# A fused decoder layer: the running maximum of the memory cell by four broadcast DMAs, the causal mask on GpSimd, and straight code in place of a loop

## The chip, the cores and the metric

The kernel runs on one core of one Trainium2 chip. The metric is the device time of one execution in microseconds, as the median of three runs; lower is better. The engines are TensorE (PE, its weight loads PEld), VectorE (DVE), ScalarE (ACT), GpSimd (POOL) and SyncE (SP), whose queue (SPq) issues all DMAs here.

## What is computed

Sixteen sequences of 256 rows and 256 columns pass through one layer of three parts, each followed by a residual sum and a layer norm: softmax attention with 16 heads and a position bias; a memory cell (mLSTM) with 4 heads of 64, whose queries are the rows and whose keys and values are a second input; and a gated feed-forward part with quantised rows and ternary weights. The change is in the memory cell. The reference has there, cut:

```python
log_fg = jax.nn.log_sigmoid(fg)
cs = jnp.cumsum(log_fg, axis=2)
log_D = where(ltr, cs - swapaxes(cs, 2, 3), -inf) + swapaxes(ig, 2, 3)
max_log_D = jnp.max(log_D, axis=-1, keepdims=True)
D = jnp.exp(log_D - max_log_D)
C = (qh @ kh.T / sqrt(DH)) * D
normalizer = maximum(abs(sum(C, -1)), exp(-max_log_D))
h = C / (normalizer + EPS) @ vh
```

With a = ig - cs and m the running maximum of a, the exponent is a[t] - m[s] for t up to s, and nothing otherwise. So each head needs its row m, 256 numbers on one SBUF partition, spread over all 128 partitions.

## The kernel before, in words

The work of a sequence (called a batch, B is 16) is spread over four or five passes of one body, so that in one pass the engines serve batches n2 = b + 2 (projections), n = b + 1, b (attention scores and softmax), c = b - 1 (end of attention, gates of the memory cell), f = b - 2 (memory cell, begin of the feed-forward part), e = b - 3 (its end) and d = b - 4 (store). Each engine has a `body` (SP L331, POOL L505, PE L834, ACT L1149, DVE L1591) that is a list of steps in an order written out by hand; between the engines stand only semaphores. Every engine is in order, so a step that waits holds up all that stands behind it in its list.

`iterations` (L247) runs the bodies: passes -1 to 3 and 14 to 19 are straight code, passes 4 to 13 are five rounds of a hardware loop with two bodies in it (`Fori`, L251). At the end of a round each engine branches back; the loop's waits are against register values.

A softmax tile (one head, 128 of its 256 rows) goes through `scores` (PE, L582), `biased` (DVE, L1311: bias and row maximum), `negated` (row tile 0 on ACT L947, row tile 1 on POOL L434), `turned` (PE transposes, L598), `exponentials` (ACT, L959) and `values` (PE, L615). There are two PSUM banks for scores, two for the turned tiles, one for values, and three that all other products share in the order of the list `uses` (L208): `lease` makes a product wait until the last user of its bank is done.

The memory cell of a batch: `mem_gates` (PE) and `gate_rows`, `gate_logs` (ACT, L984, L997) give input and forget gates as 4 rows of 256. `forget_logs` (DVE, L1500) forms the log of the forget gate, `forget_sums` (L1507) its running sum, `input_rows` (L1516) a, `running_max` (L1523) m, `max_rows` (L1530) the exponents for the normalizer. Then m is cut into three bfloat16 parts: `max_high` (L1537), `max_rest` (L1544), `max_mid` (L1552), `max_low` (L1559) on DVE, and `max_mid_copy` (L1010) on ACT. For each head `mem_decay` (PE, L702 to L705) spreads -m over 128 partitions by a product of these parts with a selecting matrix, and adds -1e30 above the diagonal by two products of the identity with `causal`. `mem_weights` on ACT (L980, L981) takes the exponential out of PSUM with a as its bias, `mem_weights` on DVE (L1490) multiplies it into the product of `mem_scores` (PE, L717), and `mem_values` (PE, L734) follows. Later come `head_stats`, `head_moments`, `head_scale`, `head_norm` (DVE), `head_rstd`, `mem_scaled`, `mem_residual` (POOL), and the feed-forward part: `row_max` (DVE, L1393), `quantised_rows`, `rows_turned`, `gate_proj`, `up_proj`, `gated`, `gated_up`, `inner_max`, `inner_scale`, `scaled`, `inner_quantised`, `down`, `ffn_residual`.

SP issues per pass the store, the second input (`load_ctx`, L318), the rows two batches ahead (`load_x`, L311), twelve SBUF to SBUF transfers of 128 KB each that stack the parts of queries and keys into 16 partitions each (`load_stack`, L305), and the residual rows `xb` (`load_residual`, L324), to which POOL adds a bias (`residual_in`, L501) for `attention_residual` (DVE, L1588).

Of the kernel before, what the change touches and what calls it, by code (L numbers as in the profile page):

```python
# [21 lines left out]
XH, XD = 4, 64  # L22
# [35 lines left out]
def build(nc, x, ctx, Wq, bq, Wk, bk, Wv, bv, Wo, bo, pos_bias, ig_w, ig_b, fg_w, fg_b, norm_w,  # L58
          w_gate, w_up, w_down, out):
    es = ExitStack()  # L60
    with es:
# [3 lines left out]
        def sig(name, per_batch=1):  # L65
# [5 lines left out]
        causal = sb("causal", [P, P], BF16)  # L71
        magic = sb("magic", [P, 1])
        zeros = sb("zeros", [P, 1])
        minus_half = sb("minus_half", [P, 8])
        xhead_sel = sb("xhead_sel", [96, XH, P], BF16)
# [42 lines left out]
        mm = sb("mm", [XH, 2, S])  # L118
        md = sb("md", [XH, S], BF16)
        ms = sb("ms", [96, S], BF16)  # L120
        aT = sb("aT", [P, TT, XH])
        emT = sb("emT", [P, 2, TT, XH])
        dT = sb("dT", [P, 2, 3 * P])
# [65 lines left out]
        gt_ps, gt_a, gt_v, ms_a = sig("gt_ps"), sig("gt_a", 4), sig("gt_v", 9), sig("ms_a")  # L189
        am_ps, am_a = sig("am_ps"), sig("am_a", 2)  # L190
        ar_ps, qk_ps, d_sb, c_sb, cv_ps, cv_sb = (sig("ar_ps", XH), sig("qk_ps", XH), sig("d_sb", 2 * XH),
# [17 lines left out]
            ("u2", 3, h_v, 6), ("g3", 3, h_v, 7), ("u3", 3, h_v, 8), ("ar0", 2, d_sb, 2), ("qk0", 2, c_sb, 1),  # L209
            ("ar1", 2, d_sb, 4), ("qk1", 2, c_sb, 2), ("ar2", 2, d_sb, 6), ("qk2", 2, c_sb, 3), ("cv0", 2, cv_sb, 1),  # L210
            ("cv1", 2, cv_sb, 2), ("cv2", 2, cv_sb, 3), ("ar3", 2, d_sb, 8), ("qk3", 2, c_sb, 4),
            ("ott0", 1, att_v, 3), ("ott1", 1, att_v, 4), ("cv3", 2, cv_sb, 4), ("attT", 1, attT_sb, 1),
            ("wo", 1, ln1, 1), ("hq0", 3, hq_sb, 1), ("cxT", 1, cxT_sb, 1), ("hq1", 3, hq_sb, 2), ("v", -1, v_sb, 1),
            ("y0", 3, y_v, 1), ("x1T", 1, x1T_sb, 1), ("y1", 3, y_v, 2), ("xT", -2, xT_sb, 1), ("gates", 1, gt_a, 1),
            ("q", -2, q_f, 1), ("k", -2, k_f, 1), ("xqT", 2, xq_sb, 1), ("g0", 2, h_v, 1), ("u0", 2, h_v, 2),
            ("g1", 2, h_v, 3), ("u1", 2, h_v, 4), ("g2", 2, h_v, 5), ("am", 1, am_a, 2),
# [41 lines left out]
        G_ALL = 21  # L258
# [10 lines left out]
        def _(sp):  # L269
# [7 lines left out]
            sp.wait_ge(g_set.sem, 5)  # L277
# [17 lines left out]
            def load_stack(n, par, which):  # L295
# [3 lines left out]
                wait(sp, split, n, 4 * which + 4)  # L299
# [20 lines left out]

            def load_residual(b):
                if live(b):
                    wait(sp, ln1, b - 1, 1)
                    sp.dma_start(xb[:], x[b].rearrange("(t p) d -> p t d", p=P)).then_inc(xb_in.sem, 16)  # L324

            def store(e):
                if live(e):
                    wait(sp, out_g, e, 3)
                    sp.dma_start(out[e].rearrange("(t p) d -> p t d", p=P), ot).then_inc(o_out.sem, 16)

            def body(b, par=None):  # L331
                par = b % 2 if par is None else par
                n2, n, c, d = b + 2, b + 1, b - 1, b - 4
# [13 lines left out]
        def _(pool):  # L347
# [5 lines left out]
            step(pool.memset(causal[:], 0.0))  # L353
            step(pool.memset(gate_w[:], 0.0))
            step(pool.memset(gate_b[:], 0.0))
            pool.wait_ge(g_set.sem, 3)
# [3 lines left out]
            step(pool.affine_select(out=causal[:], in_=causal[:], compare_op=ALU.is_ge, fill=-1.0e30, base=0,  # L360
                                    pattern=[[1, P]], channel_multiplier=-1))
            step(pool.memset(ones, 1.0))
            step(pool.memset(zeros[:], 0.0))
            step(pool.memset(minus_half[:], -0.5))
            step(pool.memset(xhead_sel[:], 0.0))
            step(pool.memset(ms[:], 0.0))
# [4 lines left out]
            pool.wait_ge(g_set.sem, 12)  # L371

            n = 17
            for off in (0, 32, 64):
                n += 1
                step(pool.affine_select(out=xhead_sel[:], in_=xhead_sel[:], compare_op=ALU.not_equal, fill=-1.0,
                                        base=-off, pattern=[[-1, XH], [0, P]], channel_multiplier=1))
                pool.wait_ge(g_set.sem, n)
# [23 lines left out]
            def split_high(n, which):  # L402
# [9 lines left out]
                wait(pool, split, n, 4 * which + 1)  # L412
                pool.tensor_tensor(src, src, parts[:, 0, which, :, :], ALU.subtract).then_inc(split.sem, 1)  # L413

            def split_low(n, which):
# [4 lines left out]
                wait(pool, split, n, 4 * which + 2)  # L420
                apart(pool)
                pool.tensor_scalar(parts[:, 1, which, :, :], src, 1.0, 0.0, ALU.mult, ALU.add).then_inc(split.sem, 1)
                wait(pool, split, n, 4 * which + 3)
# [13 lines left out]
            def inner_quantised(f, t):  # L437
# [3 lines left out]
                wait(pool, hr_a, f, t + 1)  # L441
# [8 lines left out]
            def output(e):  # L450
# [6 lines left out]
                wait(pool, out_g, e, 1)  # L457
                pool.tensor_tensor(nb[:, 1, :], nb[:, 0, :], rs[:, 2, :], ALU.mult).then_inc(out_g.sem, 1)
                wait(pool, out_g, e, 2)
# [7 lines left out]
            def head_rstd(f):  # L467

                if not live(f):
                    return  # L470
                wait(pool, gn_v, f, 22)
                apart(pool)
                pool.tensor_scalar(nrm[:, 6, :, :], nrm[:, 5, :, :], 1e-5, None, ALU.add).then_inc(gn_g.sem, 1)
                wait(pool, gn_g, f, 1)
                pool.tensor_tensor(nrm[:, 7, :, :], nrm[:, 6, :, :],
                                   minus_half[:, 0:TT * XH].rearrange("p (t h) -> p t h", t=TT), ALU.pow)\
                    .then_inc(gn_g.sem, 1)

            def mem_scaled(f):
# [3 lines left out]
                wait(pool, gn_v, f, 31)  # L483
# [3 lines left out]
            def mem_residual(f, par):  # L487
# [3 lines left out]
                wait(pool, gn_g, f, 3)  # L491
                pool.tensor_tensor(y2[:], y2[:], x1[:, par, :, :], ALU.add).then_inc(gn_g.sem, 1)  # L492

            def residual_in(b):
# [5 lines left out]
                wait(pool, xb_in, b, 16)  # L500
# [4 lines left out]
            def body(b, par=None):  # L505
                par = b % 2 if par is None else par
                n2, n, c, f, e = b + 2, b + 1, b - 1, b - 2, b - 3
                inner_quantised(e, 1)
                negated(b, 8)
                head_rstd(f)  # L510
                rstd(c, 0)
                mem_scaled(f)
                mem_residual(f, par)
                negated(b, 9)
                negated(b, 10)
                rstd(f, 1)
                negated(b, 11)
# [1185 lines left out]
```

## Time and profile before

| what | value |
|---|---|
| median of three runs | 857.5 us (857.29 to 859.87) |
| the profiled execution | 857.06 us |
| its span, first to last instruction | 855.3 us |
| mean granted TensorE clock | 0.924 |
| busy share of the span | PE 85%, DVE 80%, ACT 73%, POOL 55% |

The busy shares are over the whole span, with some 105 us at the start and 65 us at its end in which the passes are not full. The view by stretches (windows) gives the busy time of each engine between two moments, and the clock that was granted. As marks serve the starts of `forget_sums` (L1507), which runs once in a pass.

### The profile page before, as it was taken

What the parts mean: (1) busy time and instruction counts of PE and PEld (TensorE: products, weight loads), DVE (VectorE), ACT (ScalarE), POOL (GpSimd) and SP (SyncE); (2) the same over time, 40 slices, a digit from 0 to 9 for tenths busy, and PEclk for the clock granted to TensorE, in tenths of its full rate; (3) what the DMA queues carried; (4) which work ended last, traced back from release to release, by engine and by line L of the source; (5) the groups of instructions that cost most, each with busy time, mean ns of one, the idle gap of its engine ahead of it and who ended that gap; (6) DMA issues with size and microseconds to landing.
All of it is one profiled execution on the core that took longest, in us unless ns stands there. A gap on an engine that the chain in (4) does not pass through costs nothing.

```text
span 855.3 us, 20244 instructions
## 1 busy us (share of the span) xinstructions
PE 730.9 (85%) x5424; PEld 540.7 (63%) x5424; DVE 685.3 (80%) x2517; ACT 624.1 (73%) x1284; POOL 470.5 (55%) x777
## 2 busy tenths in 40 slices
PE   3379998998989798998999798988999889895842
PEld 3367776776858485866768485857668675653411
DVE  4755577989898889987888889997888998886843
ACT  0437868888888779895978779895978887875522
POOL 3446446566666667563656666673656673535132
PEclk8589999999999899998989999998989998998756
DMA  8867305070606052520607061501607070000000
GB/s 256 180 103 114 51 18 95 11 103 14 113 13 113 13 89 34 82 42 28 84 13 111 13 100 23 104 19 40 72 13 111 13 99 15 26 13 13 14 13 12
DMA packets 54582, 51.19 MB, mean 60 GB/s; under 512 B 6117, under 2 KB 54250, under 8 KB 54506
## 3 DMA queue, kind: packets, MB, share of 16 engines
q1 hardware_dynamic: 54506, 50.38, 33.9%
q8 instruction: 23, 0.38, 0.2%
q14 instruction: 53, 0.43, 0.2%
HBM read 21.00 MB, written 4.19 MB: 29 GB/s over the span
## 4 chain that ended last, share of the span: by engine, by line
PE 44%; DVE 17%; ACT 15%; issue 12%; POOL 9%; SPq 1%; POOLq 1%; DVEq 1%; DMA 0%; ACTq 0%
PE pT L598 7%; PE pO L615 5%; PE pS L582 3%; PE pB L655 2%; PE pA L655 2%; ACT L1002 2%; DVE sc L1311 2%; ACT sc L947 2%; DVE st L1323 2%; PE pB L717 2%; PE pC L568 2%; PE pC L717 1%; POOL rs L395 1%; POOL y L492 1%; ACT att L1060 1%
## 5 line engine op out<-in xcount | busy, mean ns | idle before, releaser
L434 POOL TENSOR_SCALAR sc<-sc,mx 128x256 f32<-128x256 f32 x256 | 129.0, 508 | 190.8 <-DVE mx L1311 187.5
L1311 DVE CUSTOM_DVE_ANT_0 sc<-pS,bias 128x256 f32<-128x256 f32 x512 | 199.0, 417 | 40.0 <-PE pS L582 33.5
L598 PE MATMUL pT<-ident,sc 128*128 128x128 f32 x1024 | 159.3, 280 | 28.0 <-ACT sc L947 19.0
L959 ACT ACTIVATE pr<-pT 128x512 f32<-128x512 f32 x256 | 149.5, 597 | 31.3 <-PE pT L598 30.2
L598 PEld LDWEIGHTS pT<-ident,sc 128*128 128x128 f32 x1024 | 119.2, 143 | 63.8 <-ACT sc L947 39.3
L947 ACT ACTIVATE sc<-sc,mx 128x256 f32<-128x256 f32 x256 | 124.0, 507 | 0.6 <-DVE mx L1311 0.2
L582 PE MATMUL pS<-ks,qs 96*128 96x256 bf16 x512 | 97.1, 277 | 5.8 <-DVE mx L1311 5.7
L615 PE MATMUL pO<-pr,va 128*32 128x256 f32 x1024 | 76.4, 421 | 0.0
L582 PEld LDWEIGHTS pS<-ks,qs 96*128 96x128 bf16 x512 | 43.4, 99 | 34.5 <-DVE mx L1311 20.8
L446 POOL TENSOR_SCALAR hq<-h 128x512 bf16<-128x512 f32 x64 | 38.4, 617 | 44.1 <-ACT h L1137 43.8
L411 POOL TENSOR_SCALAR parts<-qk_f 128x512 bf16<-128x512 f32 x32 | 20.6, 644 | 67.7 <-ACT qk_f L1105 66.2
L969 ACT ACTIVATE oT<-pO 128x256 f32<-128x256 f32 x64 | 24.2, 378 | 36.2 <-PE pO L615 36.2
L1049 ACT ACTIVATE x<-y,shift,rs 128x256 f32<-128x256 f32 x64 | 34.8, 591 | 16.9 <-POOL shift L399 16.3
L615 PEld LDWEIGHTS pO<-pr,va 128*32 128x32 f32 x1024 | 28.5, 116 | 23.8 <-issue 12.2
L1137 ACT ACTIVATE h<-h,magic,hs 128x1024 f32<-128x1024 f32 x32 | 40.0, 1248 | 4.8 <-DVE hs L1470 4.8
L1323 DVE BATCH_NORM_STATS2 st<-y 128x6 f32<-128x256 f32 x96 | 36.1, 419 | 8.7 <-POOL y L492 7.5
L1311 DVE DVE_READ_ACCUMULATOR2_ANT mx<- 128x1 f32 x512 | 41.3, 81 | 0.0
L424 POOL TENSOR_TENSOR parts<-qk_f,parts 128x512 bf16<-128x512 f32 x32 | 38.7, 1210 | 2.7
L413 POOL TENSOR_TENSOR qk_f<-qk_f,parts 128x512 f32<-128x512 f32 x32 | 38.3, 1196 | 2.7
L1452 DVE TENSOR_REDUCE hs<-h 128x1 f32<-128x1024 f32 x32 | 38.8, 1213 | 0.0
L395 POOL TENSOR_TENSOR rs<-ve,minus_half 128x2 f32<-128x2 f32 x48 | 35.5, 740 | 1.4
L631 PE MATMUL pB<-xT,wqT 128*128 128x256 f32 x128 | 32.3, 397 | 2.8 <-ACT xT L1096 2.8
(282 smaller groups left out, 1925.4 us busy)
## 6 DMA issues: line engine op xcount, KB each, us to landing
qs<-parts SPq DMA_DIRECT2D x96, 128.0 KB, 4.5
ks<-parts SPq DMA_DIRECT2D x96, 128.0 KB, 6.0
xin<-in_x SPq DMA_DIRECT2D x16, 256.0 KB, 3.5
bias<-in_L_attn_pos_bias SPq DMA_DIRECT2D x4, 1024.0 KB, 20.4
xb<-in_x SPq DMA_DIRECT2D x16, 256.0 KB, 6.3
cx<-in_ctx SPq DMA_DIRECT2D x32, 128.0 KB, 2.1
out<-hq SPq DMA_DIRECT2D x16, 256.0 KB, 2.2
sc<-in_L_ffn_w_gate SPq DMA_DIRECT2D x1, 1024.0 KB, 5.6
```

The source lines that it names most:

```text
L395: pool.tensor_tensor(rs[:, which, :], ve[:, which, :], minus_half[:, 0:TT], ALU.pow)\
L424: pool.tensor_tensor(parts[:, 2, which, :, :], src, parts[:, 1, which, :, :], ALU.subtract)\
L434: pool.tensor_scalar(sc[:, s % RING, 1, :], sc[:, s % RING, 1, :], -1.0, mx[:, s % RING, 1:2], ALU.mult, ALU.add).then_inc(neg_g.sem, 1)
L582: ins = pe.matmul(pS[s % 2][:, t * S:t * S + S], qs[par][:, s, t * P:t * P + P], ks[par][:, s, :], start=True, stop=True)
L598: ins = pe.transpose(bank[:, kt * S + t * P:kt * S + t * P + P], sc[:, s % RING, t, kt * P:kt * P + P], ident[:])
L615: ins = pe.matmul(pO[32 * j:32 * j + 32, 0:S], va[par][:, kt, hd, :], pr[:, hd % RING, kt, :], start=(kt == 0), stop=(kt == TT - 1))
L947: act.activation(sc[:, s % RING, 0, :], sc[:, s % RING, 0, :], ACT.Identity, bias=mx[:, s % RING, 0:1], scale=-1.0).then_inc(neg_a.sem, 1)
L959: act.activation(flat(pr[:, s % RING, :, :]), pT[s % 2][:, :], ACT.Exp, scale=-1.0)\
L1137: act.activation(h[:, t, :], h[:, t, :], ACT.Identity, bias=magic[:, :], scale=hs[:, 4, t:t + 1])\
L1311: dve.tensor_tensor_reduce(out=sc[:, s % RING, t, :], in0=pS[s % 2][:, t * S:t * S + S], in1=bias[:, t, s, ::-1], scale=1.0, scalar=LOW, o ...
L1323: dve.bn_stats(st[:, which, t, :], y[:, t, :]).then_inc(signal.sem, 1)
L1452: dve.tensor_reduce(hs[:, 0, t:t + 1], h[:, t, :], AX.X, ALU.max, apply_absolute_value=True)\
```

## The change

The running maximum m is no longer cut and multiplied: SP reads each head's row of `mm` 128 times into `mb`, by one DMA of 128 KB for each head. `mem_late` and `mem_weights` on ACT take the exponential in `mb` itself (scale -1), and POOL's `mem_causal` sets to zero what lies above the diagonal. `forget_logs` goes: ACT's `gate_rows` has a Relu more, and the running sum takes both rows. `mem_decay`, the four cutting steps, `max_mid_copy` and their tiles go, with the `ar` entries of `uses`. All batches are straight code, all waits are constants, and all five orders, and `uses`, are new. POOL's body is written one pass later against the others (its c is the b of the body of DVE that runs at the same time).

```diff
-            for b in range(-1, 4):
+            for b in range(-1, B + 4):
                 body(b)
-            with eng.Fori(2, B // 2 - 1) as pair:
-                body(pair * 2, 0)
-                body(pair * 2 + 1, 1)
-            for b in range(B - 2, B + 4):
-                body(b)
...
+            def spread_max(c):
+                if live(c):
+                    sp.wait_ge(gt_v.sem, gt_v.at(c, 3))
+                    wait(sp, c_sb, c - 1, XH)
+                    for hh in range(XH):
+                        sp.dma_start(mb[:, hh, 0:S], mm[hh:hh + 1, :].unsqueeze(1).to_broadcast([1, P, S])).then_inc(mb_in.sem, 16)
...
             def body(b, par=None):
...
-                store(d)
-                load_ctx(c)
-                load_x(n2, par)
+                spread_max(f)
+                load_x(n2, par)
+                load_residual(c)
+                store(d)
                 load_stack(n, 1 - par, 0)
                 load_stack(n, 1 - par, 1)
-                load_residual(b)
+                load_ctx(c)
...
+            def mem_causal(c, hh):
...
+                pool.wait_ge(d_sb.sem, d_sb.at(c, 2 * hh + 2))
+                apart(pool)
+                both = mb[:, hh, :].rearrange("p (b q) -> p b q", b=3)[:, 0::2, :]
+                pool.affine_select(out=both, in_=both, compare_op=ALU.is_ge, fill=0.0, base=0,
+                                   pattern=[[0, 2], [1, P]], channel_multiplier=-1).then_inc(d_sel.sem, 1)
...
+            def mem_late(c, hh):
...
+                if hh == 0:
+                    act.wait_ge(am_a.sem, am_a.at(c, 2))
+                    act.wait_ge(mb_in.sem, mb_in.at(c, 16 * XH))
+                act.activation(mb[:, hh, S:S + P], mb[:, hh, P:S], ACT.Exp, bias=aT[:, 1, hh:hh + 1], scale=-1.0)\
+                    .then_inc(d_sb.sem, 1)
...
+                act.wait_ge(d_sb.sem, d_sb.at(c, 2 * hh + 1))
+                act.activation(mb[:, hh, 0:S], mb[:, hh, 0:S], ACT.Exp, bias=aT[:, 0, hh:hh + 1], scale=-1.0)\
                     .then_inc(d_sb.sem, 1)
...
                 act.activation(sp[r, :], gt[r, :], ACT.Abs).then_inc(gt_a.sem, 1)
...
+                act.activation(gt[r, :], gt[r, :], ACT.Relu, scale=-1.0).then_inc(gt_a.sem, 1)
...
-                dve.tensor_tensor_scan(cs[:, :], sp[r, :], zeros[r, :].to_broadcast([XH, S]), 0.0, ALU.add, ALU.add)\
-                    .then_inc(gt_v.sem, 1)
+                dve.wait_ge(gt_a.sem, gt_a.at(c, 5))
+                dve.tensor_tensor_scan(cs[:, :], gt[r, :], sp[r, :], 0.0, ALU.add, ALU.add).then_inc(gt_v.sem, 1)
...
+                wait(dve, mb_in, c - 1, 16 * XH)
+                dve.tensor_tensor_scan(mm[:, :], am[z, :], am[z, :], LOW, ALU.max, ALU.max).then_inc(gt_v.sem, 1)
...
+                dve.wait_ge(d_sel.sem, d_sel.at(c, hh + 1))
```

The stretches of the new orders that bear on the broadcasts, from the step that makes m on. DVE, end of its body: forget_sums(c), input_rows(c), running_max(c), biased(b, 14, 0), row_max(f), row_max_bounded(f), row_scale(f), biased(b, 14, 1), biased(b, 15, 0), quantised_rows(f), biased(b, 15, 1), row_stats(e, 2), max_rows(c), four of biased(n, 0 and 1), row_moments(e, 2), biased(n, 2, 0), gated(f, 0), gated_up(f, 0), gated(f, 1), biased(n, 2, 1), biased(n, 3, 0), gated_up(f, 1), gated(f, 2), biased(n, 3, 1), inner_max(f, 0), two of biased(n, 4), gated_up(f, 2), biased(n, 5, 0), gated(f, 3), inner_scale(f, 0), biased(n, 5, 1), mem_weights(c, 0). Before, the cell's rows stood after biased(b, 15, 1), among the steps of gated.

POOL's whole body:

```diff
+                mem_causal(e, 3)
+                negated(c, 4)
+                inner_quantised(d, 0)
+                negated(c, 5)
+                rstd(f, 0)
+                inner_quantised(d, 1)
+                negated(c, 6)
+                head_rstd(e)
+                negated(c, 7)
+                negated(c, 8)
+                negated(c, 9)
+                mem_scaled(e)
+                mem_residual(e, 1 - par)
+                negated(c, 10)
+                rstd(e, 1)
+                negated(c, 11)
+                negated(c, 12)
+                negated(c, 13)
+                negated(c, 14)
+                split_high(n, 0)
+                split_low(n, 0)
+                negated(c, 15)
+                rstd(d, 2)
+                split_high(n, 1)
+                negated(b, 0)
+                negated(b, 1)
+                output(d)
+                residual_in(c)
+                negated(b, 2)
+                mem_causal(f, 0)
+                mem_causal(f, 1)
+                split_low(n, 1)
+                mem_causal(f, 2)
+                negated(b, 3)
```

ACT's body begins with heads_copy(c, 2), exponents(f), negated(b, 2), exponentials(b, 0), gate_tanh(e, 3), mem_late(f, 0), mem_weights(f, 0), mem_late(f, 1), mem_weights(f, 1), mem_late(f, 2), heads_copy(c, 3), mem_weights(f, 2), exponentials(b, 1). PE's body has mem_scores(f, 0) after scores(b, 6), turned(b, 2) and mem_scores(f, 1) behind it, then mem_values(f, 0); mem_gates(c) stands before scores(b, 11), where it stood after turned(b, 9).

## Rows read from the trace of the kernel before

**Rows 1.** The page's busy time of each engine over the whole span.
```profile
PE 730.9 (85%) x5424; PEld 540.7 (63%) x5424; DVE 685.3 (80%) x2517; ACT 624.1 (73%) x1284; POOL 470.5 (55%) x777
```

**Rows 2.** Windows by pass: us, then busy PE, PEld, DVE, ACT, POOL, PEclk, DMA share, GB/s.
```profile
190.51:235.31 44.80, 42.27 (x342) 31.85 (x334) 40.94 (x155) 38.19 (x81) 29.08 (x48) 1.00 0.35 61
...
235.31:279.87 44.56, 42.24 (x342) 31.88 (x334) 41.06 (x155) 38.41 (x81) 28.84 (x48) 1.00 0.34 61
...
279.87:329.32 49.45, 44.82 (x342) 33.20 (x334) 41.28 (x155) 38.34 (x81) 28.85 (x48) 0.93 0.35 54
...
373.88:424.16 50.28, 45.41 (x342) 33.66 (x334) 41.28 (x155) 38.45 (x81) 28.90 (x48) 0.93 0.35 53
...
424.16:471.84 47.68, 45.37 (x342) 33.85 (x334) 41.20 (x156) 38.36 (x81) 28.77 (x48) 0.93 0.36 55
...
471.84:520.36 48.52, 43.96 (x342) 32.61 (x334) 41.26 (x156) 38.46 (x81) 28.91 (x48) 0.96 0.34 55
```

**Rows 3.** Timeline at the end of a loop round: start us, us, engine, line, idle before.
```profile
295.76 0.56 DVE L1490 SCALAR_TENSOR_TENSOR cT<-pB,dT 128x384 f32<-128x384 f32 x1 [2.47 <-issue]
...
296.38 0.40 PE L702 MATMUL pB<-ms,xhead_sel 68*128 68x256 bf16 x1 [2.31 <-DVE cT L1490]
...
296.86 0.48 POOL L434 TENSOR_SCALAR sc<-sc,mx 128x256 f32<-128x256 f32 x1 [3.23 <-DVE mx L1311]
```

**Rows 4.** Windows, just behind that end.
```profile
296.00:298.00 2.00, 1.62 (x6) 1.22 (x7) 2.00 (x7) 0.87 (x3) 0.48 (x1) 0.50 0.02 4
```

**Rows 5.** Groups by line on DVE: busy us, mean ns.
```profile
L1537 DVE CAST ms<-mm 4x256 bf16<-4x256 f32 x16 | 14.7, 917 | 0.0
...
L1559 DVE TENSOR_TENSOR ms<-mm,md 4x256 bf16<-4x256 f32 x16 | 8.5, 530 | 0.5
...
L1500 DVE SCALAR_TENSOR_TENSOR sp<-gt,sp 4x256 f32<-4x256 f32 x16 | 7.4, 461 | 1.5 <-ACT sp L1002 1.0
...
L1544 DVE TENSOR_TENSOR mm<-mm,ms 4x256 f32<-4x256 f32 x16 | 6.8, 427 | 0.0
...
L1507 DVE TENSOR_TENSOR_SCAN cs<-sp,zeros 4x256 f32<-4x256 f32 x16 | 22.1, 1381 | 0.5
...
L1452 DVE TENSOR_REDUCE hs<-h 128x1 f32<-128x1024 f32 x32 | 38.8, 1213 | 0.0
```

**Rows 6.** The chain of waits, a stretch on PE: start us, us.
```profile
203.41 0.22 PE pC L702
203.62 0.06 PE pC L703
```

**Rows 7.** DMA view of 219 to 222 us, within the stack transfers.
```profile
DMA packets 497, 0.45 MB, mean 150 GB/s; under 512 B 57, under 2 KB 497, under 8 KB 497
```

**Rows 8.** DMA issues: KB each, median us from issue to landing.
```profile
xb<-in_x SPq DMA_DIRECT2D x16, 256.0 KB, 6.3
...
cx<-in_ctx SPq DMA_DIRECT2D x32, 128.0 KB, 2.1
```

**Rows 9.** Timeline of DVE, one pass: start us, us.
```profile
418.04 0.69 DVE L1393 TENSOR_REDUCE fs<-x 128x2 f32<-128x512 f32 x1 [0.74 <-ACT x L1049]
...
426.62 0.68 DVE L1523 TENSOR_TENSOR_SCAN mm<-am 4x256 f32<-4x256 f32 x1
...
437.51 0.55 DVE L1490 SCALAR_TENSOR_TENSOR cT<-pB,dT 128x384 f32<-128x384 f32 x1
```

**Rows 10.** Groups by line on ACT.
```profile
L980 ACT ACTIVATE dT<-pA,aT 128x256 f32<-128x256 f32 x32 | 15.4, 482 | 0.7 <-PE pA L705 0.7
```

**Rows 11.** Groups by line on POOL.
```profile
L434 POOL TENSOR_SCALAR sc<-sc,mx 128x256 f32<-128x256 f32 x256 | 129.0, 508 | 190.8 <-DVE mx L1311 187.5 <-issue 0.5
...
L501 POOL TENSOR_TENSOR xb<-xb,bo_bc 128x512 f32<-128x512 f32 x16 | 21.1, 1318 | 0.0
```

**Rows 12.** Timeline of DVE near the end of the kernel.
```profile
792.13 0.68 DVE L1523 TENSOR_TENSOR_SCAN mm<-am 4x256 f32<-4x256 f32 x1
...
801.25 0.56 DVE L1490 SCALAR_TENSOR_TENSOR cT<-pB,dT 128x384 f32<-128x384 f32 x1 [0.50 <-PE pB L718]
```

More of the change, by code:

```diff
@@ L298, in load_stack @@
                 st_, order = ((qs, Q_PARTS), (ks, K_PARTS))[which]
-                wait(sp, split, n, 4 * which + 4)
+                sp.wait_ge(split.sem, split.at(n, 4 * which + 4))
                 if which == 0:
@@ L577, in scores @@
                 if s == 0:
-                    wait(pe, stack, b, 16 * 12)
+                    pe.wait_ge(stack.sem, stack.at(b, 16 * 12))
                 if not (isinstance(lin, int) and lin < 2):
@@ L906, in body @@
                 gate_proj(f, 2)
-                exponents_turned(c)
+                turned(b, 15)
                 values(b, 2, par)
-                scores(n, 3, 1 - par)
             pe.wait_ge(v_set.sem, V_BC)
@@ L1000, in gate_logs @@
                     return
[L1001 removed]
+                act.wait_ge(gt_a.sem, gt_a.at(c, 4))
                 act.activation(sp[r, :], sp[r, :], ACT.Ln, bias=1.0).then_inc(gt_a.sem, 1)
[L1004 to L1010 removed]
             def exponents(c, par):
@@ L1150, in body @@
                 par = b % 2 if par is None else par
-                n2, c, f, e = b + 2, b - 1, b - 2, b - 3
-                exponentials(c, 14)
-                negated(c, 15)
-                gate_tanh(e, 2)
+                n2, n, c, f, e = b + 2, b + 1, b - 1, b - 2, b - 3
+                heads_copy(c, 2)
                 exponents(f, par)
-                negated(b, 0)
+                negated(b, 2)
+                exponentials(b, 0)
                 gate_tanh(e, 3)
-                max_mid_copy(f)
@@ L1159, in body @@
-                negated(b, 1)
-                heads_copy(c, 2)
-                exponentials(c, 15)
-                exponentials(b, 0)
+                mem_late(f, 0)
                 mem_weights(f, 0)
+                mem_late(f, 1)
                 mem_weights(f, 1)
-                negated(b, 2)
+                mem_late(f, 2)
+                heads_copy(c, 3)
+                mem_weights(f, 2)
+                exponentials(b, 1)
                 negated(b, 3)
+                mem_out(f, 0)
@@ L1167, in body @@
+                scaled(e, 0)
+                mem_late(f, 3)
+                mem_weights(f, 3)
                 negated(b, 4)
-                mem_weights(f, 2)
+                mem_out(f, 1)
+                attention_copy(c)
                 negated(b, 5)
-                heads_copy(c, 3)
-                mem_out(f, 0)
-                mem_out(f, 1)
-                scaled(e, 0)
-                exponentials(b, 1)
                 mem_out(f, 2)
-                mem_weights(f, 3)
                 scaled(e, 1)
+                exponentials(b, 2)
@@ L1202, in body @@
-                gate_rows(c)
+                x_copy(n2)
+                negated(b, 10)
+                exponentials(b, 8)
+                normed(f, 1, par)
+                negated(b, 11)
+                exponentials(b, 9)
+                q_copy(n2)
+                heads_copy(b, 0)
                 quantised(f)
-                gate_logs(c)
-                q_copy(n2)
+                negated(b, 12)
+                exponentials(b, 10)
+                k_copy(n2)
+                negated(b, 13)
@@ L1217, in body @@
                 exponentials(b, 13)
+                negated(n, 0)
+                gate_tanh(f, 2)
+                exponentials(b, 14)
+                exponentials(b, 15)
+                negated(n, 1)
             act.wait_ge(v_set.sem, V_BC)
```

515 lines of the change are left out of this document (199 added, 316 removed).

## The prediction

> **What bounds the kernel now.** I read the page first [rows 1]: TensorE (PE) is busy for 85% of the span and VectorE (DVE) for 80%, and these shares hold the start and the tail. So the second view is windows of one pass each [rows 2]. The reader is to see two things. In an undisturbed pass of 44.8 us PE is busy for 42.3 and DVE for 40.9; ScalarE (ACT) has 6.6 us to spare and GpSimd (POOL) 15.7. Both of the first two nearly set the pass, and since each engine is in order, a wait of one soon holds up the other. And the passes are not alike: the same work, with the same busy DVE, takes 44.8, 49.5, 50.3, 47.7 or 48.5 us, and each long one has a granted clock below 1.00. Two more, like those of 50.3 and 47.7, follow later, so there are six long passes: four that cross the end of a loop round, and two of 47.7 inside a round.
>
> The third view is the timeline where a round ends [rows 3]: DVE waits 2.47 us for nothing that the profile shows ("issue"), PE 2.31 us for DVE and POOL 3.23 us. Right behind it the granted clock is 0.50, so TensorE runs at 1.2 instead of 2.4 GHz [rows 4]. The branch costs twice: the stop, and then the clock.
>
> **Straight code.** The excess over 44.8 of the four passes with a round's end is 4.7, 5.5, 3.7 and 5.4 (the last is one that repeats the second) [rows 2], together 19.3 us. The two inside a round cost 2.9 each, 5.8 us, with no stop before them, only the low clock; I count more than half of that, since a straight order may fall into it too. I take 23 us off; the ends are 0 (the stop comes from something other than the branch) and 25. The waits against registers that become constants I cost at nothing: the clean pass inside the loop takes 44.6 us, the one that comes out of straight code 44.8 [rows 2].
>
> **What DVE loses.** Five steps go: 0.92 + 0.53 + 0.46 + 0.43 in a pass [rows 5], and `max_mid`, a cast of four rows that I take at 0.3, under the shortest of these: 2.65 us; neighbours overlap a little, so 2.4 us. The running sum stays at 1.4 us [rows 5], if its new second row costs what the zeros cost. DVE's 40.9 us become 38.5.
>
> **What PE loses.** `mem_decay` is one matmul of 256 columns and three of 128 per head, at most 0.22 + 3 x 0.06 = 0.40 us in the chain [rows 6], 1.6 us for four heads. PE has 42.3 in 44.8 us, so at 40.7 it is no longer the nearer bound, and I price the pass by DVE. Fewer leases on the three shared banks I cost at nothing.
>
> **ACT and POOL.** ACT gives up `max_mid_copy` and takes a Relu of the same few rows: nothing. Exponentials out of SBUF instead of PSUM: the same 0.48 us [rows 10]. POOL gets four selects of 256 elements; like its `negated` at 0.51 us [rows 11] they add 2.0 to 29.1 busy us, which its idle time covers. But a head's select now lies between ACT and DVE, 0.5 us on the way to each product.
>
> **The broadcasts.** No row shows a DMA that reads one partition 128 times. Bounds for the 4 x 128 KB = 0.52 MB: if it runs like the stack transfers, 150 GB/s [rows 7], 3.5 us. Those write to 16 partitions; if the rate went with the number of partitions on the narrow side, a sixteenth of it, 56 us. The ends are far apart, and neither row is nearer; I take the geometric middle, 14 us, 37 GB/s. The latency is that of a small load: 128 KB land in 2.1 us [rows 8], some 0.5 of them data at the rate of a full load, so 1.6. The rows land 15.6 us after m is made.
>
> How much time does the new order give? Before, m ends at 427.3 and the first product stands at 437.5 [rows 9]: 10.2 us, too short. In the new order m comes just ahead of the steps that begin with `row_max`, at 418.0 in the same rows, and the first product closes the pass. Of these 19.5 us go the 2.65 of the removed steps, 2.6 for the running sum, a and m, which now come first, and 0.7 for one `gated_up`. `inner_max` at 1.2 us [rows 5], `inner_scale`, `row_stats` and one `biased` come in, 3.1 us together. That gives DVE 16.6 us.
>
> ACT needs 0.9 for the two exponentials of the first head and POOL 0.5 for its select: 17.0, so 0.4 us late. **But POOL stands behind another DMA.** SP issues `load_x` and `load_residual` behind the broadcasts on the same queue, and POOL's list has `residual_in` and `negated(b, 2)` ahead of the first select. That the queue is served in order shows in `xb`: 256 KB behind the stack land after 6.3 us, where `cx` needs 2.1 [rows 8]. Two times 256 KB, at the like rate of about 0.55 us for 128 KB, are 2.2 us more, `residual_in` 1.3, `negated` 0.5, the select 0.5 [rows 11]: 15.6 + 4.5 = 20.1, that is 3.5 us late. Behind POOL's wait stand `negated(b, 2)`, all selects and `split_low(n, 1)`; for them wait PE's `turned(b, 2)`, DVE's products and, much later, the second half of the stack, which has most of a pass. Behind ACT's own wait stand `heads_copy(c, 3)` and `exponentials(b, 1)`. The wait of `running_max` for the last broadcasts and SP's for the last product are old by then and cost nothing; `load_ctx`, moved behind the stacks, waits for the cell's last product as before, 2.1 us ahead of a use some 8 PE steps later.
>
> **The pass.** DVE 38.5 + 3.5 late + 1.6 of its old 3.9 us of idle time (the waits on ACT in the feed-forward part stay, the rest is taken in by the new one) = 43.6, 1.2 us less. With 14 passes full enough: 16.8 us. PE idles less at one stretch than it did at a round's end, since `values(c, 3)`, scores and `gate_proj(e, 3)` don't hang on the late product; I take the clock as staying up.
>
> **Start and tail.** POOL's shorter setup gains nothing: DVE's first copy waits there for a small DMA. In the tail m ends at 792.8 and the first product starts at 801.3, 8.4 us later [rows 12]; now it is 17.1, 8.7 more. Against it the gates and m come before the feed-forward steps, by up to the 8.6 us between `row_max` and m [rows 9], of which I take 6. Tail: 3 us longer.
>
> **Sum.** Against the profiled execution's 857.06 us (span 855.3, so 1.8 around it, and 0.4 under the median of 857.5): 857.1 - 23 - 16.8 + 3 = 820.3; I say 820.
>
> **Rivals.**
> *The flight is too long (slower).* If the four broadcasts need 20 us of data time, a sixth of the stack's rate each being about 26 GB/s, the first select ends at 26.1, 9.5 us late; the pass is 38.5 + 9.5 + 1.6 = 49.6, and with the clock falling as in the rows, 2.9 more [rows 2], 52.5. Fourteen times 7.7, less 23, plus 8 in the tail: 950. The place is ACT's `mem_late` of the first head and POOL's `residual_in`. It decides from a pass of 46.2 us on, (23 - 3)/14 above 44.8: that is 6.1 us late, data time 16.6 us, or already at my own 14 us if the clock falls with it (43.6 + 2.9 = 46.5, total 861). For it: one row feeds everything, and a stop of 2.3 us was enough for the clock. Against: 10 us of gap became 17. Chance 0.21.
>
> The Trainium skill, SBUF — State Buffer, section "Door 1: The DMA port swizzle", speaks for this rival: partitions 0 to 3 share one DMA port of 27.2 GB/s. By it the four would take 19.3 us, an estimate, and the sum would be 898 us with the clock up and 939 with it down. By the same page 16 partitions reach about 109 GB/s; the trace's stack transfers run at 150 [rows 7], neighbours going to different sixteens, so the trace neither bears it out nor refutes it.
>
> *Only the loop pays.* The new wait, or new ones of an order in which everything moved, eat the 2.4 us: pass 44.8, total 857 - 23 + 3 = 837. For it: PE and DVE are both near their limit. Chance 0.18.
>
> *The broadcasts are quick.* At 3.5 us of data they land 5.1 us after m and nothing waits; the pass is 38.5 and 3.3 of the old idle time, 3.0 us less: 857 - 23 - 42 = 792. Chance 0.09.
>
> *The straight code does not do what it should.* The stop is the supply of instructions, not the branch; then the 23 stay and the rest gives 843, or with the 2.4 eaten about 857. Against it: passes of straight code before and after the loop show no stop. Chance 0.04, put under no change.
>
> The forecast itself, 800 to 835, has the remaining 0.48.
>
> **Range and chances.** A measurement of this kernel can tell about 0.3% from no change, 2.6 us. Faster 0.75 (0.48 + 0.18 + 0.09), same 0.04, slower 0.21. The range reaches from 790, the quick broadcasts, to 868, which takes in the fallen clock at 14 us; left out are the long flights above and a little below, about 0.18. The forecast, both faster rivals included, has 790 to 840 as its own range.
>
> **What would show it.** Right: `mb` lands 14 to 17 us after its first issue; no idle "issue" of 2 us in a pass; passes of 43 to 44 us with clock 1.00; DVE waits 2 to 4 us before its first product, POOL before `residual_in` for a DMA. Wrong: ACT waits before the first `mem_late` for `mb` over 4 us in each pass and clocks of 0.5 behind it (flight); passes of 44.8 without such a wait (order); landing under 8 us and passes under 42.5 (quick); stops without a releaser that remain (straight code).

## The result, and the profile after

The change makes the kernel slower: 1002.7 us as the median of four runs (998.02 to 1010.78), against 858.7 for the kernel before on the same chip. The ratio is 1.168, with a 95% interval of 1.159 to 1.177. The prediction of 820 us is wrong in sign, and 1002.7 lies far above its range. What came true is the rival "the flight is too long", to which it gave 0.21.

The profiled execution took 999.46 us, with a span of 997.7. First the page of the changed kernel, its busy time and the chain that ended last:

```profile
PE 749.5 (75%) x5138; PEld 557.4 (56%) x5168; DVE 646.7 (65%) x2437; ACT 627.3 (63%) x1284; POOL 484.9 (49%) x833
...
PE 28%; DMA 25%; DVE 18%; issue 9%; POOL 8%; ACT 7%; SPq 5%; POOLq 0%; DVEq 0%; ACTq 0%
DMA mb<-mm 25%; SPq L316 5%; PE pC L653 3%; DVE y L1365 3%; PE pT L596 3%; PE pC L700 3%; DVE st L1303 2%; DVE sc L1291 2%; POOL nrm L459 2%; ACT mb L965 2%; PE pA L700 1%; PE pA L566 1%; ACT mb L957 1%; PE pB L774 1%; POOL rs L379 1%
```

DVE has 38.6 us less to do than in [rows 1] and its share fell from 80 to 65%. No engine is near full. A quarter of the chain is the flight of `mb<-mm`, the four broadcasts, and the queue that issues them (SPq) holds 5% more.

The waits name the two places (engine, tile, line, what ended the wait: us in total, times, longest):

```profile
POOL xb L495 <- DMA xb<-in_x: 139.7, 14, 14.2
...
DVE cT L1470 <- issue: 100.9, 13, 9.8
...
ACT mb L957 <- DMA mb<-mm: 85.3, 16, 8.8
```

POOL stands before `residual_in` for a DMA in 14 passes, 10 us each. ACT waits for the rows of m before its first exponential, in all 16 batches. These two are the places that the rival named. The 100.9 us of DVE carry no releaser, but they stand in front of the memory cell's products.

Now one pass, by windows (columns as in [rows 2]; the marks are the starts of `running_max`), and two stretches inside it:

```profile
436.25:491.15 54.90, 44.52 (x316) 33.21 (x317) 39.07 (x150) 38.20 (x81) 30.01 (x53) 0.88 0.55 58
...
458.00:460.00 2.00, 0.00 (x0) 0.00 (x0) 0.00 (x0) 1.46 (x4) 0.00 (x0) 0.78 1.07 370
460.00:462.00 2.00, 0.00 (x0) 0.00 (x0) 0.00 (x0) 2.00 (x6) 0.00 (x0) 0.50 1.16 178
...
464.00:466.00 2.00, 1.80 (x6) 1.41 (x7) 1.15 (x2) 0.00 (x0) 1.92 (x5) 0.50 0.21 31
```

The full passes take 53.7 to 56.5 us, where a clean one took 44.8. Between 458 and 462 PE, DVE and POOL do nothing at all, and the clock goes to 0.50, TensorE's lower level of 1.2 GHz, and is still there when work starts again.

The timeline of that pass shows the order (start us, us, engine, line, idle before):

```profile
436.25 0.72 DVE L1496 TENSOR_TENSOR_SCAN mm<-am 4x256 f32<-4x256 f32 x1
...
437.00 8.37 SPq L316 DMA_DIRECT2D mb<-mm  x4
...
445.47 4.73 SPq L301 DMA_DIRECT2D xin<-in_x  x1
...
450.25 4.82 SPq L321 DMA_DIRECT2D xb<-in_x  x1
...
458.48 0.40 ACT L957 ACTIVATE mb<-mb,aT 128x128 f32<-128x128 f32 x1 [3.71 <-DMA mb<-mm]
...
462.37 1.26 POOL L495 TENSOR_TENSOR xb<-xb,bo_bc 128x512 f32<-128x512 f32 x1 [9.80 <-DMA xb<-in_x]
...
464.56 0.56 DVE L1470 SCALAR_TENSOR_TENSOR cT<-pA,mb 128x384 f32<-128x384 f32 x1 [7.57 <-issue]
```

From the end of m (436.97) it is 21.5 us until ACT has the rows. `xb`, behind them on the queue, is there 3.9 us later, and the first product starts 27.6 us after m. SP itself stands: each of the two loads takes it 4.7 to 4.8 us to issue.

The DMA view of 440 to 457 us, while the broadcasts fly, is to be read beside [rows 7]:

```profile
DMA packets 491, 0.45 MB, mean 27 GB/s; under 512 B 48, under 2 KB 491, under 8 KB 491
```

Nearly the same number of packets and bytes as in [rows 7], at 27 instead of 150 GB/s. At 27 GB/s the four broadcasts of 128 KB are 19.4 us of data, one of them 4.9; nearly as long does SP stand at each of its two issues.

The landing times, per issue, against those of [rows 8]:

```profile
mb<-mm SPq DMA_DIRECT2D x64, 128.0 KB, 12.4
...
xb<-in_x SPq DMA_DIRECT2D x16, 256.0 KB, 11.9
```

### The profile page after: what moved, and what is told of

Read it like the earlier page. It is cut to its first block, busy times and chain, and to the rows that moved or that the text cites. A ratio compares the mean times of both kernels' runs of the same rounds, so it can differ in the third digit from the quotient of the medians.

```text
span 997.7 us, 17726 instructions
## 1 busy us (share of the span) xinstructions
PE 749.5 (75%) x5138; PEld 557.4 (56%) x5168; DVE 646.7 (65%) x2437; ACT 627.3 (63%) x1284; POOL 484.9 (49%) x833
## 4 chain that ended last, share of the span: by engine, by line
PE 28%; DMA 25%; DVE 18%; issue 9%; POOL 8%; ACT 7%; SPq 5%; POOLq 0%; DVEq 0%; ACTq 0%
DMA mb<-mm 25%; SPq L316 5%; PE pC L653 3%; DVE y L1365 3%; PE pT L596 3%; PE pC L700 3%; DVE st L1303 2%; DVE sc L1291 2%; POOL nrm L459 2%; ACT mb L965 2%; PE pA L700 1%; PE pA L566 1%; ACT mb L957 1%; PE pB L774 1%; POOL rs L379 1%
## 5 line engine op out<-in xcount | busy, mean ns | idle before, releaser
L596 PE MATMUL pT<-ident,sc 128*128 128x128 f32 x1024 | 165.6, 288 | 114.1 <-issue 73.6
L596 PEld LDWEIGHTS pT<-ident,sc 128*128 128x128 f32 x1024 | 130.1, 149 | 141.5 <-issue 89.7
L938 ACT ACTIVATE pr<-pT 128x512 f32<-128x512 f32 x256 | 147.8, 591 | 10.4 <-PE pT L596 8.5
L418 POOL TENSOR_SCALAR sc<-sc,mx 128x256 f32<-128x256 f32 x256 | 123.7, 490 | 40.0 <-DVE mx L1291 38.4
L1470 DVE SCALAR_TENSOR_TENSOR cT<-pA,mb 128x384 f32<-128x384 f32 x32 | 17.8, 558 | 135.4 <-issue 100.9
L495 POOL TENSOR_TENSOR xb<-xb,bo_bc 128x512 f32<-128x512 f32 x16 | 20.2, 1265 | 153.5 <-DMA xb<-in_x 139.7
L372 POOL TENSOR_SCALAR ve<-mv 128x2 f32<-128x2 f32 x48 | 14.9, 310 | 139.5 <-DVE mv L1313 139.5
L957 ACT ACTIVATE mb<-mb,aT 128x128 f32<-128x128 f32 x64 | 24.9, 390 | 85.3 <-DMA mb<-mm 85.3
L613 PE MATMUL pO<-pr,va 128*32 128x256 f32 x1024 | 70.2, 392 | 0.4 <-ACT oT L948 0.3
L1064 ACT ACTIVATE cv<-pA 128x130 f32<-128x130 f32 x32 | 9.0, 281 | 89.0 <-PE pA L719 89.0
L470 POOL TENSOR_SCALAR_AFFINE_SELECT mb<-mb 128x256 f32<-128x256 f32 x64 | 25.6, 412 | 69.1 <-ACT mb L965 69.1
```

Source lines behind the costliest of these rows:

```text
L418: pool.tensor_scalar(sc[:, s % RING, 1, :], sc[:, s % RING, 1, :], -1.0, mx[:, s % RING, 1:2], ALU.mult, ALU.add).then_inc(neg_g.sem, 1)
L596: ins = pe.transpose(bank[:, kt * S + t * P:kt * S + t * P + P], sc[:, s % RING, t, kt * P:kt * P + P], ident[:])
L613: ins = pe.matmul(pO[32 * j:32 * j + 32, 0:S], va[par][:, kt, hd, :], pr[:, hd % RING, kt, :], start=(kt == 0), stop=(kt == TT - 1))
L938: act.activation(flat(pr[:, s % RING, :, :]), pT[s % 2][:, :], ACT.Exp, scale=-1.0)\
```

## The experiments

The theory after the result: one partition, or the few beside each other that hold m, gives its bytes at 27 GB/s whatever their destination, and all else in the queue waits behind that. The rivals: the cost is per transfer or per byte into `mb`, wherever it is read from; or the new order, the straight code or the selects cost the time. Ten kernels were run. In the table the ratio is to the kernel before, on the same chip (its medians 858.7 to 862.0 us); the profiles are each of one execution.

| kernel | edit | median us | ratio, 95% interval |
|---|---|---|---|
| s1 | before, straight code alone | 842.7 | 0.975, 0.966 to 0.983 |
| s2 | after, loads ahead of the broadcasts | 937.5 | 1.083, 1.073 to 1.092 |
| s3 | after, two broadcasts | 840.3 | 0.973, 0.966 to 0.980 |
| s5 | after, three broadcasts | 895.0 | 1.039, 1.032 to 1.047 |
| s4 | after, m through DRAM | 831.1 | 0.962, 0.954 to 0.969 |
| s6 | after, m on partitions 0 and 64 | 851.6 | 0.986, 0.978 to 0.994 |
| s9 | after, m on partitions 0 and 32 | 1017.3 | 1.187, 1.181 to 1.193 |
| s10 | s6, loads ahead | 836.4 | 0.975, 0.972 to 0.978 |
| s7 | s4 with a loop for six passes | 851.1 | 0.986, 0.980 to 0.991 |
| s8 | s4 without the selects | 829.0 | 0.961, 0.956 to 0.967 |

### Straight code alone (s1)

```diff
-            for b in range(-1, 4):
+            for b in range(-1, B + 4):
                 body(b)
-            with eng.Fori(2, B // 2 - 1) as pair:
-                body(pair * 2, 0)
-                body(pair * 2 + 1, 1)
-            for b in range(B - 2, B + 4):
-                body(b)
```

> The kernel before with its loop written out, nothing else changed: no broadcasts, the old orders. If the stop at the end of each loop round and the low clock behind it are the branch's, the four stops go and most of the six long passes come down to 44.6 to 44.8 us: 834 us, between 832 and 840. If the stops are the supply of instructions, or a straight order falls into the low clock just as often, it stays at 850 to 858. This also says how much of the measured slowdown hides a gain: on the first theory the rest of the change costs 1003 - 834 = 169 us, not 145.

The median falls by 19 us (14 to 29 by the interval), so straight code isn't what slows the change. The 842.7 us lie above the 840 of the first expectation and below the 850 of the second. The windows of three of its passes:

```profile
243.61:288.40 44.79, 42.22 (x342) 31.88 (x334) 40.70 (x156) 38.23 (x81) 29.24 (x47) 1.00 0.37 60
146.83:195.72 48.89, 46.11 (x334) 34.51 (x334) 40.82 (x155) 38.84 (x82) 27.10 (x42) 0.90 0.28 50
557.13:605.06 47.93, 45.35 (x342) 33.89 (x334) 41.15 (x156) 38.38 (x81) 29.48 (x48) 0.93 0.33 56
```

The stops are gone, the low clock is not: four of the passes take 47.9 to 48.9 us, 3.1 to 4.1 above the clean 44.8, in code with no branch. So each of the two theories is right in part. The profiled executions differ by 10.4 us only (spans 855.3 and 844.9). The prediction took off 23.

### Other loads first (s2)

```diff
-                spread_max(f)
                 load_x(n2, par)
                 load_residual(c)
+                spread_max(f)
```

> The changed kernel, with SP issuing the rows of x and the residual rows ahead of the four broadcasts instead of behind them. Theory A (the flight, plus what stands behind it in the queue): POOL no longer waits for xb some 9 us in each pass, the first select comes right behind ACT's exponentials, 3 to 4 us earlier, so a pass falls from 54.9 to 51 or 52 us: 940 to 965 us. Theory B (only the flight counts, since ACT's wait for mb ends last): 995 to 1003 us. Theory C (the new order itself is bad): no change either.

65 us less than after (1002.7 to 937.5, the median of runs from 929 to 944 us), with not a byte less. That is a little under the 940 to 965 expected. POOL's wait for `xb` is gone, ACT's for the rows stays:

```profile
ACT mb L957 <- DMA mb<-mm: 88.6, 16, 9.0
```

So the slow transfers held up the loads behind them. That was 65 of the 171.6 us which lie between after and the best way of spreading m that was tried (s4, below), some 40%; the rest is the rows themselves. (The profiled execution is the longest of the four, 943.69 us; it is read for these waits alone.)

### Half and three quarters of the broadcasts (s3, s5)

```diff
-                    for hh in range(XH):
+                    for hh in range(2):
```

and `range(3)`, with `mb` set to zero once in the setup. s3 leaves out the running maximum of two heads, s5 that of one; ACT, POOL and DVE do the same work.

> The changed kernel with the broadcasts of heads 0 and 1 only; for heads 2 and 3 the rest runs on whatever stands in mb, so half of the running maximum is left out. Two broadcasts are 9.8 us less of data time. Theory A (flight): the rows land some 11.5 us after m instead of 21.4, xb at 15.5; the wait of about 8 us in each pass goes, and with it the low clock: passes of 43 to 45 us, 820 to 850 us. Theory C (the order is bad, or the select on POOL in the path): still above 900 us.

> The changed kernel with the broadcasts of heads 0, 1 and 2; head 3 runs on whatever stands in mb, so a quarter of the running maximum is left out. Three broadcasts have 14.7 us of data time, close to the 14 us on which the forecast of 820 us was made, so this tries the rest of its sum. If that sum is right, POOL is served its residual rows some 4 us after the rows of m and the pass is 43.4 to 46.5 us, depending on TensorE's clock: 825 to 865 us. If the rest of the sum was too kind as well, passes of 48 us and more: above 885 us. The four points (0, 2, 3, 4 broadcasts) show from where on a broadcast more is paid in full: linear from four down would be 5 us of a pass each, 921 us here.

Two, three and four broadcasts give 840, 895 and 1003 us: 55 and 108 for one more each. With two, the passes are 42.4 to 46.6 us but for the last (40.8), and ACT never waits for the rows. With three, 14.6 us of data by the rate above, the mean over its 15 passes is 47.1 us. That is nearly the data time (14 us) that the prediction took, and the kernel is 4% slower with it, not 4% faster. Two of the passes of s5, and the first product of the shorter one:

```profile
485.36:529.67 44.31, 40.99 (x318) 30.77 (x319) 38.50 (x151) 38.27 (x81) 30.00 (x53) 1.00 0.55 70
...
250.02:302.28 52.26, 47.24 (x318) 35.74 (x319) 38.90 (x150) 38.43 (x81) 30.00 (x53) 0.87 0.50 59
```

```profile
505.85 0.56 DVE L1471 SCALAR_TENSOR_TENSOR cT<-pA,mb 128x384 f32<-128x384 f32 x1 [1.14 <-issue]
```

Of its eleven full passes (204.88 to 716.11 us) five have a clock of 1.00 and take 44.3 to 45.6 us, mean 44.7; six have a lower one and take 45.1 to 52.3, mean 47.9. In the pass of 44.3 us the product starts 19.8 us after the end of m.

### Through DRAM (s4)

```diff
-                    for hh in range(XH):
-                        sp.dma_start(mb[:, hh, 0:S], mm[hh:hh + 1, :].unsqueeze(1).to_broadcast([1, P, S])).then_inc(mb_in.sem, 16)
+                    sp.dma_start(m_rows, mm[:, :]).then_inc(m_out.sem, 16)
+
+            def read_max(c):
+                if live(c):
+                    sp.wait_ge(m_out.sem, m_out.at(c, 16))
+                    src = bass.AP(tensor=m_rows.tensor, offset=0, ap=[[0, P], [S, XH], [1, S]])
+                    sp.dma_start(mb[:, :, 0:S], src).then_inc(mb_in.sem, 16)
...
                 load_residual(c)
+                read_max(f)
                 store(d)
```

m goes out as 4 KB, and one DMA reads 512 KB back, behind the two loads. As many bytes are written into `mb` as before, but none of them is read from SBUF.

> The changed kernel with another way for the running maximum: the four rows go to DRAM in one DMA of 4 KB, and one DMA of 512 KB reads them back to all partitions, issued behind the rows of x and xb. Theory A (the slow part is that one SBUF partition is read 128 times): DRAM is read at 200 GB/s or more, the rows land 6 to 9 us after m, no engine waits for them, and the pass shows what the new order is worth: 43 to 44 us, 805 to 840 us. If the slow part is a broadcast of any source, or the write into mb, the DMA of 512 KB takes as long as the four, and it stays at 980 to 1010 us. Theory C (order): above 900 us with the rows there in time.

It is the fastest of those that compute the whole result, 0.962 of before (s8, with 829.0, leaves out the mask). One pass and its timeline, then the landing time:

```profile
411.62:455.30 43.68, 41.08 (x320) 30.85 (x319) 38.48 (x151) 38.27 (x81) 30.07 (x53) 1.00 0.44 74
```

```profile
412.36 0.28 SPq L317 DMA_DIRECT2D m_rows<-mm  x1
...
413.69 0.92 SPq L323 DMA_DIRECT2D mb<-m_rows  x1
...
428.61 0.40 ACT L965 ACTIVATE mb<-mb,aT 128x128 f32<-128x128 f32 x1
...
430.89 0.56 DVE L1478 SCALAR_TENSOR_TENSOR cT<-pA,mb 128x384 f32<-128x384 f32 x1
```

```profile
mb<-m_rows SPq DMA_DIRECT2D x16, 512.0 KB, 4.9
```

Issued at 413.69, the rows are there at about 418.6, 6.3 us after m, both legs and the queue's waits included. ACT needs them at 428.6 and waits for nothing. And the first product starts 18.6 us after m: this is what the order allows. The prediction had reckoned 16.6.

Against s1, on the same chip, s4 has 11.5 us less (842.7 to 831.1): of its gain over before, more than half is straight code.

### Two places in SBUF (s6, s9, s10)

```diff
-                dve.tensor_tensor_scan(mm[:, :], am[z, :], am[z, :], LOW, ALU.max, ALU.max).then_inc(gt_v.sem, 1)
+                dve.tensor_tensor_scan(mm[z, :], am[z, :], am[z, :], LOW, ALU.max, ALU.max).then_inc(gt_v.sem, 1)
+                dve.wait_ge(gt_v.sem, gt_v.at(c, 3))
+                dve.tensor_copy(mm[64:64 + XH, :], mm[z, :]).then_inc(gt_v.sem, 1)
...
+                        row = hh + 64 * (hh % 2)
-                        sp.dma_start(mb[:, hh, 0:S], mm[hh:hh + 1, :].unsqueeze(1).to_broadcast([1, P, S])).then_inc(mb_in.sem, 16)
+                        sp.dma_start(mb[:, hh, 0:S], mm[row:row + 1, :].unsqueeze(1).to_broadcast([1, P, S])).then_inc(mb_in.sem, 16)
```

s9 has 32 in place of 64, in both lines; s10 is s6 with the order of s2. All four broadcasts are there again, of the same bytes.

> The changed kernel with the four rows of m copied by DVE to partitions 64 to 67 as well (0.3 us more in a pass); the broadcasts of heads 1 and 3 read there, those of heads 0 and 2 from partitions 0 and 2. If the 27 GB/s are the limit of the place that is read (a partition, or a port that neighbours share), the engines that run ahead into the next broadcast no longer meet the others, as in the stack transfers, and two broadcasts overlap in part: the rows land 13 to 18 us after the first issue instead of 21, 870 to 960 us. If it is a limit of a broadcast as such (of the engines that read one row again and again), nothing changes: 1000 to 1010 us.

> As the run with two places (851.6 us), but the copies that heads 1 and 3 are broadcast from stand on partitions 32 to 35 instead of 64 to 67. If the places that share a limit are neighbouring partitions only, or each partition by itself, this is as good as 64: 845 to 860 us, and 50 GB/s or more while both are read. If partitions 0 to 3 and 32 to 35 share one port, as the Trainium skill's page SBUF — State Buffer has it (Door 1: The DMA port swizzle), the copy is of no use: 27 to 28 GB/s and 995 to 1010 us.

> The run with two places (851.6 us), with the rows of x and the residual rows issued ahead of the broadcasts. The rows of m land about 12 us after m in a window of 16, so the last broadcasts may slip by the 2 to 3 us of the two loads without a wait, and POOL's short waits for xb go: 838 to 850 us. If the two loads push the broadcasts past their window, 855 to 870 us.

Windows within the broadcasts of s6, then of s9:

```profile
339.00:341.00 2.00, 1.46 (x11) 0.95 (x12) 1.97 (x6) 1.82 (x6) 1.85 (x3) 1.00 0.76 55
341.00:343.00 2.00, 0.93 (x6) 0.56 (x7) 1.97 (x12) 1.52 (x3) 0.55 (x1) 1.00 0.69 58
```

```profile
446.00:448.00 2.00, 2.00 (x18) 1.38 (x19) 1.87 (x6) 1.57 (x4) 1.92 (x5) 1.00 0.80 27
448.00:450.00 2.00, 2.00 (x24) 0.97 (x17) 1.83 (x4) 2.00 (x8) 1.22 (x3) 1.00 0.87 29
```

One copy of four rows to partition 64 doubles the rate, to 55 and 58 GB/s, and the kernel falls by 151 us, further than either theory in the expectation had it. The same copy to partition 32 leaves it at 27 to 29, and the kernel stays as slow as after. So the limit is on the side that is read, and by place: the rows on partitions 0 and 2 share one way out with those on 33 and 35, and the rows on 65 and 67 have another (these are the rows that the kernels read). By the rule of the Trainium skill, SBUF — State Buffer, section "Door 1: The DMA port swizzle", partitions 0 to 3 and 32 to 35 are on one port and 64 to 67 on another, with 27.2 GB/s for each port; the runs agree in rate and in place. What the 14.6 us by which s9 lies above after (on another chip) are made of isn't settled; its extra copy of 0.28 us and the wait before it, 16 times, are the smaller part.

With the loads ahead s10 comes to 836.4 us, 15 less than s6 and a little under the 838 to 850 expected.

### A loop in the good version (s7), and no selects (s8)

```diff
-            for b in range(-1, B + 4):
+            for b in range(-1, 6):
+                body(b)
+            with eng.Fori(3, B // 2 - 1) as pair:
+                body(pair * 2, 0)
+                body(pair * 2 + 1, 1)
+            for b in range(B - 2, B + 4):
                 body(b)
```

> The kernel that sends the running maximum through DRAM (831 us), with the loop back, over passes 6 to 13: three returns of the loop. If a return costs the stop and the low clock behind it as in the kernel before (3.7 to 5.5 us each), 840 to 850 us. If in the new order the return meets an idle moment or the clock does not fall, 831 to 836 us.

Four rounds have three returns. Each of the three passes with a return takes 51.8 or 51.9 us, 8.2 more than the clean one, and the kernel 20 us more than s4. One of them, a stretch of 2 us in it, and DVE's first instruction after the stop:

```profile
365.10:417.00 51.90, 45.77 (x318) 34.37 (x319) 38.98 (x151) 38.79 (x81) 30.13 (x52) 0.90 0.35 62
...
392.00:394.00 2.00, 2.00 (x9) 1.62 (x7) 1.35 (x7) 0.00 (x0) 0.00 (x0) 0.50 1.15 127
```

```profile
388.99 0.69 DVE L1437 TENSOR_TENSOR h<-h,pB 128x512 f32<-128x512 f32 x1 [4.13 <-issue]
```

The stop and the low clock behind it are those of [rows 3, 4], at a greater price than the 3.7 to 5.5 us of the loop before; 851.1 us is also a little more than the 840 to 850 expected.

```diff
-                both = mb[:, hh, :].rearrange("p (b q) -> p b q", b=3)[:, 0::2, :]
-                pool.affine_select(out=both, in_=both, compare_op=ALU.is_ge, fill=0.0, base=0,
-                                   pattern=[[0, 2], [1, P]], channel_multiplier=-1).then_inc(d_sel.sem, 1)
+                pool.sem_inc(d_sel.sem, 1)
```

s8 leaves out the causal mask of the memory cell.

> The kernel that sends the running maximum through DRAM (831 us), without the affine select on POOL: the causal mask is left out, and the semaphore is raised by POOL at once. Theory: the select is off the path that sets the pass, since the first product comes 18 us after m with the rows there after 6, and POOL has time; 827 to 833 us. If the select with its way ACT to POOL to DVE is what keeps the pass at 43.7 us, it falls by up to 2 us a pass: 800 to 820 us.

829.0 against 831.1 us, within the spread of both; its clean passes stay at 43.6 to 43.8. The selects, 0.41 us each and 25.6 in all, are covered.

## Why the prediction was wrong, point by point

**The step that failed** is in "The broadcasts": "neither row is nearer; I take the geometric middle, 14 us, 37 GB/s". The data time is 19.4 us at 27 GB/s, measured in after and, with the rows on the same way out, in s9. The lower end of the bounds, a fast rate from transfers that use 16 partitions, was not a neighbour of a read from one partition, and the middle between two ends 16 times apart is no measurement. The prediction's own estimate of 19.3 us by the Trainium skill stood beside the sum, as evidence for a rival.

The rest of the same chain erred the same way, by less. Rows in hand 21.5 us after m, of which 19.4 are data, leaves 2.1 for the start against 1.6. `xb` then takes 3.9 us more against 2.2. From there to the product it is 2.2 us, where 1.3 + 0.5 + 0.5 = 2.3 was forecast. Altogether 27.6 us against 20.1. Against it stands one error in the other direction: the order allows 18.6 us, not 16.6. Late by 27.6 - 18.6 = 9.0.

**The clock** is the second failed step: "I take the clock as staying up". After a stop of 7 us it was at 0.50. The pass shown adds up: 43.7 (s4) + 9.0 late = 52.7, and 2.2 are left to 54.9. That this remainder is the low clock is argued, not shown; the prediction had 2.9 for it in its rival. Nor is it the same everywhere: in the pass of 56.5 us the product starts 25.1 us after m, 6.5 late, and 6.3 are left, at a mean clock of 0.82.

s5 tests what is left of the sum when the data time is nearly the prediction's. With the clock up, its path holds: in the five passes with a clock of 1.00 the product starts 19.8 to 21.0 us after m, where the prediction had 20.1, and their mean is 44.7, 1.0 over s4. But six of the eleven full passes have a lower clock, and their mean is 47.9. The ends lose too: of the 55.2 us by which s5 lies above s4 between the first m and the last, 31 are in the first two and the last two passes. There the order allows 14.8 to 17.5 us to the product (s4), and in s5 it starts after 19.8 to 22.2. The prediction priced the full passes and, beside them, only the tail. So 14.6 us of data turn the sign with the clock and the ends as they are.

The point from which the rival decides was put at 16.6 us of data with the clock up; the 19.4 of after lie beyond it even so. With two heads (9.7 us of data) the kernel is faster than before, with three (14.6) it is slower, so the point lies between.

**The rival** had the mechanism, both places and the fallen clock right. Its 950 us is too low: passes of 52.5 where they are 54 to 56, for 14 passes where all 15 intervals between two m are long (52.7 and 50.0 at the ends too).

**Where the time is**, in the profiled executions. After lies 997.7 - 829.9 = 167.8 us above s4, which differs in how m gets to 128 partitions and in that the read stands behind the two loads. From the first m to the last, after needs 813.2 us and s4 650.7, which is 162.5, 10.8 for each of 15 passes; the tail has 6.6 of it. The start is 1.3 us shorter, which gives back the difference.

**What was right**, with the rows in time:
- DVE's busy time: forecast 38.5 us a pass, measured 38.48 in s4 (39.07 in after).
- The pass: forecast 43.6, 1.2 under 44.8. s4 has 43.7, but that is luck. The forecast had in it 3.5 us of lateness, and s4 has none. With the rows early the prediction's own terms give 38.5 + 3.3 = 41.8, and "passes under 42.5" was its sign for that case. DVE is idle for 5.2 us in the pass of s4, before the change for 3.9: of the 2.4 us taken off its work a little under half came out of the pass. Its waits there are short ones, 0.4 to 1.1 us, for ACT, PE and POOL; it is not the selects (s8), and nothing else was tried.
- The queue is served in order and POOL stands behind `xb`: s2, 65 us.
- The selects and ACT's work cost nothing: s8.
- No stop without a releaser at a round's end: s1 and s4 have none.

**What was off besides.** Straight code: 23 forecast, 19 by the medians, 10 by the profiled executions, since four passes fall to the low clock without a branch. The tail: 3 us forecast, but 71.5 us from the last m to the end in s4 against 63.2 before, 8.3 more. Of these, 6.6 lie between the end of m and the first product (15.0 against 8.4); the 6 us that the prediction took back don't show, and why wasn't tried.

So a gain was there, 30.7 us (861.9 to 831.1) in s4, which has all of the change but the four SBUF reads, where 37 were forecast: 19 of them by straight code (s1) and 11.5 by the rest. The reads, with the loads standing behind them, cost 171.6 (1002.7 - 831.1); with the loads ahead of them (s2) they cost 106.

## What to carry to other kernels

Price a broadcast by DMA by the bytes that leave the source, copies included, and by where the source lies: here 27 GB/s out of partitions 0 to 3, though all 128 are written. Spread the source over groups that don't share a way out, or send the few KB through DRAM and let one DMA read them often; and put the loads that others need soon ahead of a slow transfer on the same queue, not behind it. When the ends of a bound lie a factor of ten apart and the sign of the result depends on it, the forecast is the rival's as much as one's own.

## What the runs showed that was not expected

- A trip through DRAM was shorter than a direct one: 4 KB out and 512 KB back in 6.3 us, where four direct broadcasts needed 21.5.
- Slow transfers hold the engine that issues the next ones: SP needed 4.73 and 4.82 us to issue one load each, about the time of one broadcast. That the queue was full is our reading and isn't shown. The same issues take 0.39 and 0.46 us in s4:

```profile
412.74 0.39 SPq L303 DMA_DIRECT2D xin<-in_x  x1
413.18 0.46 SPq L328 DMA_DIRECT2D xb<-in_x  x1
```

- TensorE's clock falls in straight code too: 0.90 and 0.93 over whole passes of s1, which are 3.1 to 4.1 us longer. In the first of them PE's idle times just before are of 1.27 and 0.81 us, with no stop of 2 us. What brings the clock down there was not tried.
- The price of a loop's return isn't fixed: 3.7 to 5.5 us in the order before, 8.2 in the order of s7. What makes it dearer there was not tried.
